# Masking the attention weights on GpSimd and VectorE by turns, with value matmuls of two key tiles back to back

## The reference

```python
h = jnp.maximum(_layernorm(x, axis=-1), 0.0)
q, k, v = heads(h @ Wq + bq), heads(h @ Wk + bk), heads(h @ Wv + bv)
scores = jnp.einsum('bhqd,bhkd->bhqk', q, k) * scale
scores = jnp.where(mask[:, None] == 0, -jnp.inf, scores)
attn = jax.nn.softmax(scores, axis=-1)
out = jnp.einsum('bhqk,bhkd->bhqd', attn, v)
return x + (out.transpose(0, 2, 1, 3).reshape(b, s, D_MODEL) @ Wo + bo)
```

## Time and profile before

| | us |
|---|---|
| runs of the kernel before | 1730.51, 1732.61, 1741.83; median 1732.61 |
| the profiled execution, own time | 1734.83 |
| its span | 1733.0 |
| PE busy | 1660.5 (96%) |
| DVE busy | 1532.9 (88%) |
| ACT busy | 1473.9 (85%) |
| POOL busy | 147.1 (8%) |

### The profile page before, as it was taken

How to read it: one execution, slowest core, us unless ns; L and a number is a source line. 1 busy time by engine, 2 the same in 40 slices (tenths; PEclk the granted TensorE clock), 3 DMA queues, 4 the chain that set the end, 5 groups by cost and what they waited for, 6 DMA issues and landing times.

```text
span 1733.0 us, 27505 instructions
## 1 busy us (share of the span) xinstructions
PE 1660.5 (96%) x8000; PEld 1035.8 (60%) x8000; DVE 1532.9 (88%) x3653; ACT 1473.9 (85%) x3493; POOL 147.1 (8%) x199
## 2 busy tenths in 40 slices
PE   3899999999999999999999999999999999999987
PEld 2646566566666666666666666666666666656643
DVE  5689898999989899898999989899998999988894
ACT  2688889898898989899898988989888888988983
POOL 0000100101000011100011010010100001110010
PEclk9989999999999999999999999999999999999989
DMA  5434343433434334343333433344343333433311
GB/s 164 116 79 117 88 111 90 113 100 105 108 94 110 91 109 118 101 105 87 112 91 110 118 97 103 90 113 106 104 106 93 111 90 111 119 86 103 87 50 37
DMA packets 118677, 175.17 MB, mean 101 GB/s; under 512 B 32384, under 2 KB 34432, under 8 KB 118528
## 3 DMA queue, kind: packets, MB, share of 16 engines
q1 hardware_dynamic: 114432, 172.35, 37.2%
q10 hardware_dynamic: 4096, 1.06, 0.3%
HBM read 54.79 MB, written 16.78 MB: 41 GB/s over the span
## 4 chain that ended last, share of the span: by engine, by line
PE 76%; DVE 15%; issue 3%; SPq 3%; ACT 2%; DMA 1%; POOL 0%; POOLq 0%; DVEq 0%; ACTq 0%
PE ps L663 14%; PE psO L694 13%; PE ps L674 11%; PE psP L587 11%; PE psP L588 11%; PE psP L589 11%; DVE ps L489 4%; DVE probs L496 4%; PE ps L677 3%; PE ps L635 1%; DVE stats L416 1%; SPq L224 1%; SPq L227 1%; DVE x_tile L424 1%; DVE y_tile L520 1%
## 5 line engine op out<-in xcount | busy, mean ns | idle before, releaser
L489 DVE CUSTOM_DVE_ANT_0 ps<-ps,bias_q 128x512 f32<-128x512 f32 x1024 | 708.4, 693 | 140.2 <-PE ps L663 130.4
L346 ACT ACTIVATE ps<-ps,neg_max 128x512 f32<-128x512 f32 x1024 | 686.8, 671 | 95.9 <-DVE neg_max L489 75.7
L380 ACT ACTIVATE probs<-ps 128x512 f32<-128x512 f32 x1024 | 620.9, 607 | 74.2 <-PE ps L677 72.0
L496 DVE SCALAR_TENSOR_TENSOR probs<-bias_k,probs 128x512 f32<-128x512 bf16 x768 | 550.0, 717 | 6.7 <-ACT probs L380 6.7
L663 PE MATMUL ps<-k_stack,q_stack 96*128 96x512 f32 x1024 | 451.3, 441 | 16.5 <-ACT ps L346 7.8
L674 PE MATMUL ps<-q_stack,k_stack 98*128 98x512 f32 x1024 | 413.8, 405 | 5.1 <-ACT probs L380 4.6
L663 PEld LDWEIGHTS ps<-k_stack,q_stack 96*128 96x128 f32 x1024 | 194.2, 190 | 273.2 <-ACT ps L346 127.6
L694 PE MATMUL psO<-probs,v_sb 128*32 128x512 f32 x2048 | 276.9, 613 | 1.9 <-DVE oT_lo L509 0.9
L674 PEld LDWEIGHTS ps<-q_stack,k_stack 98*128 98x128 f32 x1024 | 196.6, 192 | 45.7 <-ACT probs L380 19.0
L346 ACT ACTIVATION_READ_ACCUMULATOR ps<-ps,neg_max 128x1 f32 x1024 | 217.9, 213 | 0.0
L489 DVE DVE_READ_ACCUMULATOR2_ANT neg_max<- 128x1 f32 x1024 | 143.6, 140 | 0.0
(11 more groups left out here) (60 smaller groups left out, 1920.4 us busy)
## 6 DMA issues: line engine op xcount, KB each, us to landing
q_stack<-part_hi SPq DMA_DIRECT2D x512, 64.0 KB, 2.0
k_stack<-part_hi SPq DMA_DIRECT2D x512, 64.0 KB, 2.0
x_tile<-in_x_dram SPq DMA_DIRECT2D x64, 256.0 KB, 2.9
adj_tile<-in_adj_dram SPq DMA_DIRECT2D x64, 256.0 KB, 3.0
q_stack<-part_lo SPq DMA_DIRECT2D x256, 64.0 KB, 2.0
k_stack<-part_lo SPq DMA_DIRECT2D x256, 64.0 KB, 2.0
y_tile<-in_x_dram SPq DMA_DIRECT2D x64, 256.0 KB, 2.9
out_dram<-y_tile SPq DMA_DIRECT2D x64, 256.0 KB, 2.1
```

The lines of the kernel that those rows point to most:

```text
L346: nc.scalar.activation(item, item, ACT.Exp, scale=-1.0, bias=neg_max[:, g % 2, col:col + 1], accum_out=exp_sum[:, col:col + 1]).then_inc(e ...
L380: nc.scalar.activation(probs[:, n % P_RING, :], ps2[:, n % 2, :], ACT.Exp, scale=SCALE).then_inc(exp2_done, 1)
L489: nc.vector.tensor_tensor_reduce(bank1(("s", u)), bank1(("s", u)), bias_q[:, qt, :], -SCALE, 3.0e38, ALU.add, ALU.min, neg_max[:, g % 2, c ...
L496: nc.vector.scalar_tensor_tensor(out=probs[:, n % P_RING, :], in0=bias_k[:, n % 16 // 4, :], scalar=-MASKED, in1=probs[:, n % P_RING, :], ...
```

## The change

- The mask: tiles with n % 8 in 0..3 (key tiles 0 and 2) are masked by GpSimd, as an int32 product of the bits of `probs` with `keep_k` (1 or 0); tiles with n % 8 in 4..7 (key tiles 1 and 3) by VectorE as before. The mask matmul is gone. VectorE forms `keep_k` from the transposed mask in the bank after ScalarE has copied the other half to `bias_k`.
- The value matmuls of two key tiles stand one after the other at u % 8 == 4, `probs` has nine tiles.
- The adj tiles land in the two y buffers (`adj_view`) instead of a buffer of their own; loads and the forming of `bias_q` stand at other slots, and the y loads wait for the last use.
- The m turn moves from u = 53 to 55; `oT_hi` and `oT_lo` of three of the four groups stand two slots earlier (their value matmuls too).
- GpSimd's step runs through the slots, with the masks between its other work.

```diff
@@ -25,14 +25,13 @@
-ADJ_AT = (17, 24, 30, 36)
-BIAS_AT = (24, 30, 36, 46)
+ADJ_AT = (21, 23, 29, 31)
+BIAS_AT = (27, 29, 34, 37)
...
-P_RING = 8
-VECTOR_MASKED = (0, 1, 2, 4, 5, 6)
+P_RING = 9
...
@@ -43,7 +42,7 @@
-         24: [("c", 2, -1)], 40: [("c", 3, -1)], 53: [("m", 0, 0)], 56: [("c", 0, 0)], 61: [("m", 1, 0)]}
+         24: [("c", 2, -1)], 40: [("c", 3, -1)], 55: [("m", 0, 0)], 56: [("c", 0, 0)], 61: [("m", 1, 0)]}
...
@@ -51,8 +50,8 @@
-O_HI_AT = {16: 0, 31: 1, 47: 2, 63: 3}
-O_LO_AT = {17: 0, 32: 1, 48: 2, 63: 3}
+O_HI_AT = {16: 0, 29: 1, 45: 2, 61: 3}
+O_LO_AT = {17: 0, 30: 1, 46: 2, 62: 3}
...
@@ -158,11 +157,20 @@
-        def masked_before(n):
-            return n // 8 * len(VECTOR_MASKED) + sum(i < n % 8 for i in VECTOR_MASKED)
-        MASKED_ALL = masked_before(SLOTS)
+        def prob(b, n):
+            return probs[:, (SLOTS * b + n) % P_RING, :]
+        def even_before(n):
+            return n // 8 * 4 + min(n % 8, 4)
+        def odd_before(n):
+            return n // 8 * 4 + max(n % 8 - 4, 0)
+        def adj_view(t):
+            return y_tile[:, t % 2, :].bitcast(I32)
...
@@ -185,15 +193,20 @@
-                    sp.wait_ge(bias_done, due(4 * b + t))
-                    sp.dma_start(adj_tile[:], adj_rows[bass.ds(row, 1)].rearrange("a p d -> (a p) d")
-                                 ).then_inc(adj_in, 16)
+                    if t < 2:
+                        sp.wait_ge(y_out[t], due(16 * 2 * (b - 1)))
+                    else:
+                        sp.wait_ge(bias_done, due(4 * b + t - 1))
+                    sp.dma_start(adj_view(t), adj_rows[bass.ds(row, 1)].rearrange("a p d -> (a p) d")
+                                 ).then_inc(adj_in[t % 2], 16)
+                    if t < 2:
+                        sp.wait_ge(bias_done, due(min(4 * (b + 1), 4 * (B - 1)) + t + 3))
...
@@ -286,17 +299,26 @@
+            def mask(b, n):
+                if n in (0, 8):
+                    pool.wait_ge(keep_k_done, due(2 * b + n // 8 + 1))
+                pool.wait_ge(exp2_done, due(64 * b + n + 1))
+                tile = prob(b, n).bitcast(I32)
+                nc.gpsimd.tensor_tensor(tile, tile, keep_k[:, n % 16 // 8, :], ALU.mult).then_inc(even_masked, 1)
...
...
+                for u in range(SLOTS):
+                    if u == 5: form_rstd(k, 2)
+                    if u == 10: form_rstd(k, 3)
+                    if u == 12: add_bo(k - 2, 2)
+                    if u == 14: add_bo(k - 2, 3)
+                    if u in (44, 45): form_rstd(k + 1, u - 44)
+                    if k == 0 and u == 52:
+                        pool.wait_ge(small_in, 64)
+                    if u in (52, 53): add_bo(k - 1, u - 52)
+                    b, n = pass2(k, u)
+                    if have(b) and n // 4 % 2 == 0:
+                        mask(b, n)
...
@@ -374,10 +396,10 @@
-                        if n % 4 == 0:
-                            act.wait_ge(pv_done, due(16 * b + n // 4 - 1))
+                        if (n - P_RING) % GROUP == 0:
+                            act.wait_ge(pv_done, due(16 * b + (n - P_RING) // GROUP + 1))
...
-                        nc.scalar.activation(probs[:, n % P_RING, :], ps2[:, n % 2, :], ACT.Exp, scale=SCALE
+                        nc.scalar.activation(prob(b, n), ps2[:, n % 2, :], ACT.Exp, scale=SCALE
...
@@ -391,11 +413,9 @@
-                            act.wait_ge(scores2, due(64 * (k - 1) + 48 + 8 * n + 8))
-                            act.wait_ge(probs_masked, due(MASKED_ALL * (k - 1) + masked_before(48 + 8 * n + 8)))
-                            nc.scalar.activation(bias_k[:, 2 * n:2 * n + 2, :], bank1((kind, n, rel)).bitcast(BF16).rearrange("p (t q) -> p t q", q=S),
-                                                 ACT.Identity).then_inc(m_done, 1)
+                            act.wait_ge(odd_masked, due(32 * (k - 1) + odd_before(48 + 8 * n + 8)))
+                            nc.scalar.activation(bias_k[:, n, :], bank1((kind, n, rel)).bitcast(BF16)[:, S:2 * S], ACT.Identity
+                                                 ).then_inc(bias_k_done, 1)
...
@@ -456,6 +476,11 @@
+                elif kind == "m":
+                    dve.wait_ge(bias_k_done, due(2 * b + n + 1))
+                    dve.wait_ge(even_masked, due(32 * (b - 1) + even_before(48 + 8 * n + 8)))
+                    nc.vector.tensor_scalar(keep_k[:, n, :], bank1((kind, n, rel)).bitcast(BF16)[:, 0:S], 0.0, None, ALU.is_equal
+                                            ).then_inc(keep_k_done, 1)
...
@@ -490,12 +515,14 @@
-                    if have(b) and n % 8 in VECTOR_MASKED:
...
+                    if have(b) and n // 4 % 2 == 1:
+                        if n in (4, 12):
+                            dve.wait_ge(bias_k_done, due(2 * b + n // 8 + 1))
...
-                        nc.vector.scalar_tensor_tensor(out=probs[:, n % P_RING, :], in0=bias_k[:, n % 16 // 4, :], scalar=-MASKED,
-                                                       in1=probs[:, n % P_RING, :], op0=ALU.add, op1=ALU.min
-                                                       ).then_inc(probs_masked, 1)
+                        nc.vector.scalar_tensor_tensor(out=prob(b, n), in0=bias_k[:, n % 16 // 8, :], scalar=-MASKED,
+                                                       in1=prob(b, n), op0=ALU.add, op1=ALU.min
+                                                       ).then_inc(odd_masked, 1)
...
@@ -646,6 +674,23 @@
+            def weigh_values(b, n, parity):
+                g, kt = n // 4, n % 4
+                if kt == 0:
+                    pe.wait_ge(o_hi_done, due(4 * b + g))
+                    pe.wait_ge(o_lo_done, due(4 * b + g))
+                if g == 0:
+                    pe.wait_ge(v_done, due(4 * b + kt + 1))
+                pe.wait_ge(even_masked, due(32 * b + even_before(4 * n + 4)))
+                pe.wait_ge(odd_masked, due(32 * b + odd_before(4 * n + 4)))
+                for j in range(GROUP):
+                    at = DH * (GROUP * g + j)
+                    last = nc.tensor.matmul(psO[32 * j:32 * j + 32, :], v_sb[:, parity, kt, at:at + DH],
+                                            prob(b, 4 * n + j), start=(kt == 0), stop=(kt == NT - 1))
+                last.then_inc(pv_done, 1)
...
@@ -668,32 +713,13 @@
-                        if g == 0 and j == 0:
-                            pe.wait_ge(m_done, due(2 * b + kt // 2 + 1))
-                        last = nc.tensor.matmul(ps2[:, n % 2, :], k_stack[:, g, j, P * kt:P * kt + P], q_stack[:, g, j, :],
-                                                start=True, stop=(n % 8 in VECTOR_MASKED))
-                        if n % 8 not in VECTOR_MASKED:
-                            last = nc.tensor.matmul(ps2[:, n % 2, :], ident_b[:], bias_k[:, kt, :], start=False, stop=True)
-                        last.then_inc(scores2, 1)
+                        nc.tensor.matmul(ps2[:, n % 2, :], k_stack[:, g, j, P * kt:P * kt + P], q_stack[:, g, j, :],
+                                         start=True, stop=True).then_inc(scores2, 1)
...
-                    if u % 4 == 2 and have(k - 1):
...
+                    if u % 8 == 4 and have(k - 1):
+                        for n in (u // 8 * 2, u // 8 * 2 + 1):
+                            weigh_values(k - 1, n, 1 - parity)
```

41 lines of the change are left out of this document (9 added, 32 removed).

## The result

The changed kernel takes 1835.55 us (median of 4 runs, 1831.22 to 1838.37), the kernel before on the same chip 1735.38: a ratio of 1.0566 with the 95% interval 1.0532 to 1.0601. It is slower by 100 us. The forecast was 1773 us and its range ended at 1815, so the direction was right and the size was not.

The account below looks back on a forecast made before the run. TensorE, nearly dense at 96% busy, was taken as the bound. Floor 94.3 + last mask 6.4 + port 3.0 + mask turn 2.0 = 105.7 us a block, 2.6 above 103.1, giving 1773 us, range 1698 to 1815.

Parts of the forecast that it names:

- The floor of 94.3 us a block: Block time of 103.1 us less mask matmuls 3.7, merging 2.6 and old TensorE waits 2.5, before added waits.
- GpSimd's mask at 1.3 us: Each of GpSimd's 32 masks a block was taken to cost 1.3 us, like its add of the same shape.
- The wait for VectorE's last mask, 6.4: Second value group waits for VectorE's mask of the last tile; 6.4 us a block summed over eight windows.
- The turn of the mask: Mask transposes at u=55, directly before the c turn: waits of 1.25 at slot 56, 0.5 at 57; 2.0 us in all.
- the merging under "What goes away": Two value groups back to back pay entry and exit once, saving 8 x 0.33 = 2.6 us a block.
- The VectorE time that was saved lies in slots 5 to 8, where nobody waits for it: In each eight-slot window ending with the values at slot 12, VectorE's saved time was said to help no wait.
- the port priced inside the windows alone: GpSimd masks holding VectorE's: 3.0 us a block, at u=12 (1.1), 20 (0.4), 44 (0.4) and 52 (1.1).
- 105.7: Forecast block time in us: floor 94.3, last-mask waits 6.4, port 3.0 and mask turn 2.0.
- its own range: The forecast's narrower range, from 1.0 us a block less to 1.8 more: 1752 to 1802 us.
- the faster one: Rival: port collisions fall beside value matmuls, VectorE's waits absorb the turn's; 101.1 us a block, 1701 us; chance 0.27.
- The rule of the shared port: Only VectorE instructions in 2-port mode or with two SBUF inputs contend with GpSimd; maxima, statistics and y sums pass freely.

Follow-up runs that it names:

- the run with narrow GpSimd masks: The changed kernel with GpSimd masking only the first 64 of 512 columns of its tiles: 1796.96 us, ratio 1.0339.
- the unpaired run: The changed kernel with value matmuls one key tile at a time at u % 4 == 2, oT_hi/oT_lo at their old slots: 1834.51 us, ratio 1.0551.
- eleven tiles: The changed kernel with eleven exponential tiles, value pairs at u % 8 == 6, bo left out, bf16 keep_k with float product: 1785.49 us, ratio 1.0293.
- four edits: The changed kernel with last mask before maximum, first mask turn at 53, h turns at 3 and 11, bias and normalise moved: 1718.28 us, ratio 0.9911.

## Why the prediction was wrong

**Right.** The floor of 94.3 us a block: the measured slots, with their waits taken out, come to about 94. GpSimd's mask at 1.3 us: 1.29. The wait for VectorE's last mask, 6.4: the run with narrow GpSimd masks, in which the port hardly counts, has 6.6, window by window within 0.4 but for slot 4, where 0.7 was put and none came. The turn of the mask, down to its two waits: 2.0 forecast, 2.7 by the run with the turn at 53, of which some 0.5 is half clock behind it.

**The step that failed, by size,** is the merging under "What goes away". It prices the value groups that move by their own length alone and puts at nothing, without a reason, what they covered where they stood. The groups at slots 2, 6, 10, 14 and 62 used to follow the transposes at 1, 5, 10, 13 and 61, and gave the ring of three banks time to turn. Without them slots 1, 2, 5, 6, 10, 11, 13, 14, 61 and 62 hold about 2.9 us a block beyond a plain slot, after 0.36 for the transposes of an h, 0.44 for those of the mask and 0.1 behind a pair are taken off. Two runs show a part of it: moving the transposes from 5 to 3, under a pair, gives 0.5 back, and in the unpaired run slots 61 to 2 take 0.8 less, its two groups taken off. That the rest of the 2.9 is cover is read from the slots and not shown.

**The step that failed, by mechanism,** is "The VectorE time that was saved lies in slots 5 to 8, where nobody waits for it", and with it the port priced inside the windows alone. Slots 5 to 8 of a window are when GpSimd masks. Whatever of `bias_q`, a normalise or the three small operations of c VectorE has there stands up to 1.3 us, and three score banks later TensorE can stand too. Slots 39 and 50 lose 1.6 us together with narrow masks and 1.8 with bias and normalise moved. With 0.3 of slot 55 the port outside the windows is 1.85. Inside them the 3.0 were 0.3 (slot 12). Over the eleven blocks only two VectorE masks of a block are held, both taken in slot 12, for 0.84 us together (0.52 with narrow masks: the same 0.3); no VectorE operation of slots 17 to 20, 41 to 44 and 49 to 51 is, since GpSimd had ended before VectorE's first mask there (by 0.2 us at slots 17 and 49 of the block around 800 us). By size the two halves nearly cancel (1.85 against 2.7), so this step alone would not have made the forecast too low.

Added up, against 105.7: last mask +0.2, port inside -2.7, port outside +1.85, lost cover +2.9, turn +0.7, make 108.65; the 0.65 up to the measured 109.3 is in small pieces that I did not assign. That the port's share of the sum comes out near is luck: it was priced at the wrong places, and the two errors largely offset each other. Fifteen and a half blocks of the missing 3.6 us are 56 of the 63 us by which the forecast was short. (The lower edge of its own range, 1.0 us a block less, is 1757 and not 1752.)

Of the rivals, the faster one credited waits with giving VectorE time to catch up. That is right as a mechanism (unpaired values, eleven tiles), but it works against the gain too: part of a wait removed comes back at the next tight place, here mostly slots 55 to 58, and with half clock behind it.

The rule of the shared port (the Trainium skill, GPSIMD Engine Reference, section Specifications) names VectorE instructions in a 2-port mode or with two SBUF inputs. Where a row can test it, the trace of the changed kernel agrees: masks, with two inputs from SBUF, were held, and a maximum (L514 at 810.19, 0.69 us beside the GpSimd pair of 808.69), with one of its two inputs in a score bank, was not, nor were the statistics (at most 0.70 us). `bias_q` and normalise were held too; they have one tile input each, and no row shows in which mode they ran.

What stays open: how much of the 2.9 us is cover, and whether a ring of eleven without the wait for the exponential would keep the 7 us.

## What to carry to other kernels

When matmuls are moved, price also what they covered where they stood: here a turn of h through a ring of three banks cost nothing more under a pair of groups and about half a microsecond ahead of a plain slot, and the turn of the mask 2.7 us at the wrong slot. When work goes to an engine that shares a port, list what the neighbour runs in the same slots, small operations too, and follow each late one around the buffer ring to where it is waited for; and price a collision only in the slots where both engines really have work at the same time. Move one thing at a time to find the places, but judge them together: four edits that gave 5.95 us a block alone gave 7.7 at once.

## What the runs showed of the hardware

Waits of TensorE of a microsecond or two can cost twice. Around the 2.25 us wait of the unpaired run the windows read, columns as above:

```profile
875.00:877.00 2.00, 0.00 (x0) 0.00 (x0) 2.00 (x3) 0.30 (x1) 1.64 (x3) 0.89 0.00 0
877.00:883.00 6.00, 5.88 (x19) 3.21 (x20) 2.51 (x7) 2.42 (x6) 2.38 (x2) 0.50 0.24 87
883.00:884.00 1.00, 1.00 (x5) 0.78 (x5) 0.73 (x2) 0.60 (x2) 0.00 (x0) 0.81 0.00 0
```

TensorE did nothing from 875 to 877, then ran at 0.50, the 1.2 GHz level, for over 6 us with full work, and then at 2.4 GHz again. In 2 us windows over 60 to 1700 us the unpaired run has 123 us at half clock, the run with bias and normalise moved 68, the changed kernel 24 and the kernel before 27 (all at the run's two ends). The changed kernel, whose waits are as long but a little differently placed, has only two such stretches in its middle, of 6 to 8 us each: 7 us of its 100 at most.

A VectorE operation of 16 columns, 0.18 us by itself, is held for up to 1.27 us by one GpSimd instruction: its size gives it no better place.
